# First layer's projection weights loaded in the causal half, low parts shared by two engines

## The reference, cut to what matters

```python
h = _layernorm(x) * (1 + ca) + sa
x = x + ga * attn_ref(h, Wq, Wk, Wv, Wo)          # causal half
h = _layernorm(x) * (1 + cb) + sb
for i in range(DEPTH):                            # DEPTH = 6
    x = attn_layer(shift_tokens(x), Wqkv[i], q_scale[i], k_scale[i], Wo[i]) + x
    x = ffn_layer(shift_tokens(x), ln_g[i], ln_b[i], W1[i], b1[i], W2[i], b2[i]) + x
x = x + gb * h                                    # h now: the six layers' result
```

## Time and profile before

| | us |
|---|---|
| median of 3 runs | 3825.32 (3816.24 to 3826.53) |
| the profiled execution's own time | 3833.82 |
| its span, first to last instruction | 3832.0 |
| mean granted TensorE clock | 0.981 |

### The profile page before, as it was taken

How to read it: one execution, slowest core, us unless ns; L and a number is a source line. 1 busy time by engine, 2 the same in 40 slices (tenths; PEclk the granted TensorE clock), 3 DMA queues, 4 the chain that set the end, 5 groups by cost and what they waited for, 6 DMA issues and landing times. The chain is left out here.

```text
span 3832.0 us, 147280 instructions
## 1 busy us (share of the span) xinstructions
PE 3621.4 (95%) x64322; PEld 2756.7 (72%) x64322; DVE 3100.3 (81%) x4927; ACT 2455.5 (64%) x3855; POOL 2310.7 (60%) x1367
## 2 busy tenths in 40 slices
PE   6888888599999999999999999999999999999996
PEld 4666665477777777777777777777777777777774
DVE  4554454699988899989899989988899998889893
ACT  4555555367666667666667666666666766666663
POOL 1001000677777677777677777776777777777771
PEclk9999999799999999999999999999999999999998
DMA  1000000222222222222222222212222222221112
GB/s 56 4 4 4 4 7 7 64 54 56 54 56 54 68 54 56 54 56 60 61 54 56 54 63 62 56 53 56 54 68 54 56 54 54 57 57 52 52 52 70
DMA packets 122998, 188.79 MB, mean 49 GB/s; under 512 B 25054, under 2 KB 44278, under 8 KB 122108
## 3 DMA queue, kind: packets, MB, share of 16 engines
q1 hardware_dynamic: 122364, 179.36, 17.3%
HBM read 24.08 MB, written 4.19 MB: 7 GB/s over the span
## 5 line engine op out<-in xcount | busy, mean ns | idle before, releaser
L1308 POOL TENSOR_TENSOR rc<-rc,rnorm 128x1024 f32<-128x1024 f32 x384 | 731.4, 1905 | 394.5 <-DVE rnorm L170 377.4
L1302 POOL TENSOR_TENSOR rc<-rc,rs 128x1024 f32<-128x1024 f32 x384 | 910.6, 2371 | 7.2 <-DVE rs L1367 3.6
L1343 POOL TENSOR_TENSOR prob_b<-prob_b,rinv 128x1024 f32<-128x1024 f32 x192 | 365.4, 1903 | 358.3 <-DVE rinv L1448 358.2
L1361 DVE TENSOR_TENSOR rc<-proj,rope_b 128x1024 f32<-128x1024 f32 x384 | 465.6, 1212 | 87.1 <-ACT squares L1165 85.9
L1165 ACT ACTIVATE squares<-proj 128x1024 f32<-128x1024 f32 x384 | 392.7, 1023 | 181.5 <-PE proj L917 178.0
L1008 PEld LDWEIGHTS ring<-pT,vmoved 64*64 64x64 f32 x18432 | 380.3, 135 | 136.1 <-issue 136.1
L1367 DVE TENSOR_TENSOR rs<-proj,rope_b 128x1024 f32<-128x1024 f32 x384 | 466.1, 1214 | 0.0
L1375 DVE TENSOR_REDUCE sums<-squares 128x16 f32<-128x1024 f32 x384 | 463.9, 1208 | 0.0
L954 PEld LDWEIGHTS ring<-ident,rc 128*128 128x128 f32 x3072 | 361.5, 141 | 138.9 <-issue 43.5
L737 DVE TENSOR_REDUCE negmax<-tm 128x1 f32<-128x384 f32 (+3 forms) x352 | 222.3, 639 | 285.3 <-PE tm L421 285.0
L954 PE MATMUL ring<-ident,rc 128*128 128x128 f32 x3072 | 428.7, 277 | 12.2 <-POOL rc L1308 9.7
(11 more groups left out here) (172 smaller groups left out, 8027.4 us busy)
## 6 DMA issues: line engine op xcount, KB each, us to landing
vmoved<-vown SPq DMA_DIRECT2D x576, 128.0 KB
vmoved<-vown SPq DMA_DIRECT2D x192, 192.0 KB
vmoved<-vown SPq DMA_DIRECT2D x576, 64.0 KB
wqkv_raw<-in_L_ffn_Wqkv SPq DMA_DIRECT2D x40, 192.0 KB, 3.4
wo<-in_L_ffn_Wo SPq DMA_DIRECT2D x6, 512.0 KB, 4.8
x_attended<-xtok SPq DMA_DIRECT2D x8, 256.0 KB, 2.0
xtok_c<-x_attended SPq DMA_DIRECT2D x8, 256.0 KB, 4.4
out<-xtok_c SPq DMA_DIRECT2D x8, 256.0 KB, 2.8
```

What stands on the lines that cost most here:

```text
L1302: nc.gpsimd.tensor_tensor(rc[:, k % 2, c, :], rc[:, k % 2, c, :], rs[:, c, :], ALU.add).then_inc(add_done, 1)
L1308: nc.gpsimd.tensor_tensor(dst, dst, rnorm[:, k % 2, c * HEADS:(c + 1) * HEADS].rearrange("p (h o) -> p h o", o=1).broadcast_to([P, HEADS, ...
L1343: nc.gpsimd.tensor_tensor(pr, pr, rinv[:, :, :].rearrange("p q (s o) -> p q s o", o=1).broadcast_to([P, PAIRS, 2, KEYS]), ALU.mult).then_i ...
L1361: nc.vector.tensor_tensor(rc[:, k % 2, c, :].rearrange("p (h d) -> p h d", h=HEADS), proj[c][:, :].rearrange("p (h d) -> p h d", h=HEADS), ...
```

## The change

`first_raw` becomes a buffer of its own (128 x 3072 float32, 12 KB in each partition), allocated outside the blocks, so that it lives through `part_a` and `part_b`. In `part_a` its first 2560 columns serve as `sel_raw`. As soon as both readers of `sel_raw` are done, SP issues one DMA of the whole 128 x 3072 matrix into it and waits for its landing before the first store of `x_attended`. In `part_b` the eight chunk loads and ScalarE's wait for them are gone, the counts of `raw_in` are lower by eight, GpSimd makes the low parts of chunks 0, 2, 4 and 6, and VectorE those of 1, 3, 5 and 7. The number of DMA issues falls by seven; nothing else changes in number.

```diff
@@ program
+        first_raw = sb("first_raw", [P, QKV])
@@ part_a
-        sel_raw = sb("sel_raw", [P, 20, P])
+        sel_raw = first_raw[:, 0:20 * P].rearrange("p (s f) -> p s f", s=20)
@@ part_a, SyncE
             sp.dma_start(xtok[:, :, :], xv).then_inc(x_in, 16)
+            sp.wait_ge(sel_d, 1)
+            sp.wait_ge(wo_p, 1)
+            sp.dma_start(first_raw[:, :], t_in["L0_ffn_Wqkv"][0, :, :]).then_inc(ahead_in, 16)
+            sp.wait_ge(ahead_in, 16)
             for b in range(BATCH):
@@ part_b
-        first_raw = oT[:, :, :].rearrange("p q t -> p (q t)")
@@ part_b, SyncE
             load_qks(0)
-            for s in range(BATCH):
-                chunk = slice(s * WCHUNK, (s + 1) * WCHUNK)
-                sp.dma_start(first_raw[:, chunk], wqkv[0, :, chunk]).then_inc(raw_in, 16)
             load_wo(0)
@@ part_b, ScalarE
-            act.wait_ge(raw_in, 16 * BATCH)
             for s in range(BATCH):
                 split_hi(s, first_raw[:, s * WCHUNK:(s + 1) * WCHUNK])
...
-                    act.wait_ge(raw_in, 16 * (i + 1))
+                    act.wait_ge(raw_in, 16 * (i - BATCH + 1))
@@ part_b, GpSimd
-            for s in range(BATCH):
+            for s in range(0, BATCH, 2):
                 split_lo(s, first_raw[:, s * WCHUNK:(s + 1) * WCHUNK])
@@ part_b, VectorE
+            for s in range(1, BATCH, 2):
+                chunk = slice(s * WCHUNK, (s + 1) * WCHUNK)
+                dve.wait_ge(w_hi_done, s + 1)
+                nc.vector.tensor_tensor(w_lo[:, 0, chunk], first_raw[:, chunk], w_hi[:, 0, chunk].bitcast(f32),
+                                        ALU.subtract).then_inc(w_lo_done, 1)
             for g in STEPS:
```

More of the change, by code:

```diff
@@ L122, in program @@
         vecs = sb("vecs", [P, VECS, DEPTH])
+        first_raw = sb("first_raw", [P, QKV])
         x_attended = nc.dram_tensor("x_attended", (P, BATCH * TILES, DIM), f32, kind="Internal").ap()
-        part_a(nc, t_in, alloc, need, x_attended, resT, ident, masks, mod, vecs)
-        part_b(nc, t_in, alloc, need, resT, ident, win_mask, ident_bf, vecs)
+        part_a(nc, t_in, alloc, need, x_attended, resT, ident, masks, mod, vecs, first_raw)
+        part_b(nc, t_in, alloc, need, resT, ident, win_mask, ident_bf, vecs, first_raw)
         part_c(nc, out, alloc, need, x_attended, resT, ident, mod)
@@ L233, with part_a @@
 NORMS = norm_order()
-def part_a(nc, t_in, alloc, need, x_attended, resT, ident, masks, mod, vecs):
+def part_a(nc, t_in, alloc, need, x_attended, resT, ident, masks, mod, vecs, first_raw):
     f32, f32r, bf16 = mybir.dt.float32, mybir.dt.float32r, mybir.dt.bfloat16
@@ L288, in part_a @@
         loaded = sem("loaded")
-        x_in = sem("x_in"); kept = sem("kept")
+        x_in = sem("x_in"); kept = sem("kept"); ahead_in = sem("ahead_in")
         tr_w = sem("tr_w"); tr_v = sem("tr_v"); ev_w = sem("ev_w"); silu_d = sem("silu_d")
@@ L739, in _, with part_b @@
                                             negate=True).then_inc(max_d, 1)
-def part_b(nc, t_in, alloc, need, resT, ident, win_mask, ident_bf, vecs):
+def part_b(nc, t_in, alloc, need, resT, ident, win_mask, ident_bf, vecs, first_raw):
     f32, f32r, bf16 = mybir.dt.float32, mybir.dt.float32r, mybir.dt.bfloat16
```

## The result

| | before | changed |
|---|---|---|
| median of 20 runs, us | 3828.33 | 3817.72 |
| profiled execution, us | 3833.82 | 3821.76 |
| its span, us | 3832.0 | 3819.8 |

The ratio of the changed kernel to the one before is 0.9976, with a 95% interval of 0.9967 to 0.9985: 0.24% faster, as forecast (the two medians by themselves lie 10.6 us or 0.28% apart). Timed again, beside three variants, it was 0.9982 (0.9970 to 0.9995). In the second series of variants one run of the kernel before took 9191.68 us, at a granted clock of 0.595, and stands in no ratio.

The account below looks back on a forecast made before the run. The handover path to TensorE's first product was taken as the bound: 677.65 + 3.80 + 2.0 + 1.75 = 685.2 against 694.28, a gain of 9.1 us, so 3816.2 from the median 3825.3; range 3806 to 3826.

Parts of the forecast that it names:

- (2): At the handover, subtractions wait for the rotary table's load and start at 677.65, 3.75 us after the first issue.
- (3): At the handover, GpSimd's four subtractions take 0.95 us each, 3.80 us.
- (5): At the handover, VectorE's four subtractions cost GpSimd their full four times 0.5 us, 2.0 us; lower bound 0.
- (6): At the handover, the tail from L1277 to TensorE's first product stays unchanged at 1.75 us.
- Term (8): In the loop, order stays unchanged on every engine; VectorE's four subtractions end 7 us or more before its first turn.
- term (4): At the handover, VectorE's 128x384 subtraction takes about 555 ns, back to back about 0.5 us; alone, four are off the path.
- Rival A: At the handover, the two engines' halves overlap: TensorE starts at 683.2, gain 11.1 us, time 3814.2; chance 0.22.
- 3137.7 us within 2: From TensorE's first product to the kernel's end, the time stays at 3137.7 us within 2 us, or the forecast is wrong.
- Rival B: In the ramp, TensorE's clock rises earlier after the shorter pause: gain 11.5 us, time 3813.8; chance 0.12.
- Rival C: In the causal half, the early load is in the way: gain 5.4 us, time 3819.9; chance 0.10.
- term (7): In the causal half, the early load meets the `xtok` transfer: costed at nothing, upper bound 3.7 us after slack.
- Rival D: In the loop of 192 tiles, L1387's mean rises to 634 ns: slower by 4.5 us, 3829.8; chance 0.08.

Follow-up runs that it names:

- three variants: The changed kernel with all eight low parts on VectorE (0.9976 to before), also without the table wait (0.9968), also input first and products by chunk (0.9967).
- the sharing alone: The kernel before, loads where they were, with chunks 1, 3, 5 and 7 on VectorE: GpSimd's first subtraction to first product 6.83 us, ratio 0.9999.

## Why the prediction was right

The forecast was 3816.2 for the median and a fall of 0.24%; measured were 3817.72 and 0.24%. Step by step, in us from the block's first issue:

| step | forecast | measured |
|---|---|---|
| ScalarE starts | 1.7 | 1.54 |
| (2) subtractions start | 3.75 | 3.76 |
| (3), (5) GpSimd's four with the turns | 5.8 | 4.74 |
| (6) tail to the first product | 1.75 | 2.08 |
| first product | 11.3 | 10.58 |
| first product to the end | 3137.7 | 3137.5 |

The start was exact: the table's load took 3.7 us, against 3.6 beside the raw loads. Term (5) was right in kind and too large: 2.0 forecast, 0.94 among the four and 0.33 more in the tail that term (6) called unchanged, nearly all of it in the copy of L1277 (0.52 us in place of 0.20), so 1.27 in all. I had charged each VectorE instruction with its pace of 0.5 us, and it cost GpSimd 0.31: in turns a pair takes 1.27 us, where GpSimd's alone come every 0.95 and VectorE's every 0.47, together 1.42. Term (8) had VectorE's four end 7 us or more before its first turn; it was 5.6 (680.73 to 686.34), and enough. For term (4), a VectorE subtraction by itself, 555 ns was read between two rows and 546 measured. The Trainium skill's rule (SBUF — State Buffer, "SBUF: two separate sides") says that the port pair is held for the whole instruction. The turns agree with it. What the prediction made of it, a full 0.5 us for each instruction, came out at 0.31 when GpSimd was the loser. Whether the hold is shorter than the instruction or the two overlap at their starts isn't shown, since the records of one engine overlap too: VectorE's take 546 ns and come every 469.

Rival A (no turns) gave 9.3 for the first product and 5.6 for the sharing alone, against 10.58 and 6.83: it is out. Its total, 3814.2, was nearer to the forecast than the runs can tell, so only the stretches decide. The same holds for the agreement of the totals, which is in part luck. The interval, 0.15 to 0.33%, holds A's 0.29 and B's 0.30 as well, and the sign "3137.7 us within 2" came true in this profile only: the changed kernel's second profile has 3127.7 there, the second of the kernel before 3144.8. What is right beyond luck is the handover, 9.1 forecast and 9.0 to 9.8 measured. Rival B didn't happen. The stretches that answer to the earlier trace rows:

```profile
680.00:685.00 5.00, 2.65 (x6) 2.15 (x7) 0.73 (x1) 0.00 (x0) 4.77 (x10) 0.50 0.15 44
685.00:690.00 5.00, 3.94 (x12) 2.69 (x11) 3.66 (x4) 3.22 (x5) 1.62 (x2) 0.76 0.00 0
```

The granted clock was at half (1.2 GHz) when TensorE started. It didn't rise earlier than before: all twelve products of the first projection came one every 0.43 us, where in the kernel before the last three followed after 0.32, 0.23 and 0.23. The six before the first turn were slow in both, and from first product to first turn there are 3.99 us against 4.17. Rival C didn't happen: VectorE's first read of `xtok` came at 24.43 and not later, 7.91 us behind TensorE's first matmul (16.52) as in the kernel before (17.43 and 25.34), so the early load delayed nothing, though it took 6.6 us to land where term (7) had 4.6 as its upper bound. Rival D didn't either: L1387's mean is 569 ns (before 563), its median 633 (634), its longest 1974 (1786):

```profile
L1387 DVE TENSOR_SCALAR sums<-sums 128x32 f32<-128x32 f32 x192 | 109.3, 569 | 5.0
```

Not settled is what makes the part behind the first turn scatter from 3117 to 3143 us in profiles of a loop that no kernel here changes. Of the two kernels profiled twice, the one before took 3133.6 and 3140.6 there, the changed one 3133.5 and 3123.7. The mean granted clock was 0.987 in the shortest and the third shortest and 0.983 in the three longest, but 0.981 in the fourth longest. A part of it goes with the chip or the hour: the variants were run in three series, each on another chip, and the medians of the kernel before were 3830.6, 3822.3 and 3817.4 us; the four shortest of the fourteen are the four profiles of the last series. No run was made to part these. This scatter is larger than all that was gained here, and it is why ratios so near to 1 need many runs.

## What to carry to other kernels

When a load leaves the path, look for the next semaphore on the same engine: here a table that the waiting step doesn't even use took its place, and moving that wait behind the step gave 2 us more. Before work is split over VectorE and GpSimd, look in the trace whether the two take turns in such instructions: then the faster engine alone can be quicker than both. Here the subtractions with two SBUF inputs took turns. A change of 0.2% is judged by the stretch that it touches, measured from a fixed event, and by the total only after many runs.

## What the runs showed of the hardware

A VectorE subtraction of 128x384 with both inputs in SBUF takes 0.55 us alone and 1.34 beside GpSimd's. Each makes GpSimd's take 0.31 us longer; one of 128x192 makes it 0.11. The other way round VectorE's subtraction takes 0.80 us longer than alone behind one of GpSimd's 0.99 us. With two such lists running, exactly one instruction of each passes in turn: four of GpSimd's and four of VectorE's took 5.2 us, while eight on VectorE, undisturbed, took 3.84. Two SBUF inputs aren't needed for it. The loop's L1387 has one (128x32, 0.18 us undisturbed), and in the changed kernel all 134 of its 192 that took over 0.4 us had started inside an instruction of GpSimd and ended 0.04 us behind it. L1361, with one of its two inputs in PSUM, took 1.16 to 1.23 us throughout, though GpSimd was busy at the start of 324 of its 382. Eight DMAs of 192 KB at the head of a block had their last landing scatter by 0.85 us between two executions; the one of 1.5 MB issued in the causal half landed in 6.6 us in the two profiles that were read for it.
